# Row maxima in four groups of four heads, and value products of two heads interleaved on two column groups

## What is computed

```python
h = _layernorm(x) * (1 + ca) + sa
qkv = h @ w_qkv + b_qkv                      # 16 heads, 8 channels each
att = einsum('bhqd,bhkd->bhqk', q, k) / sqrt(8)
att = softmax(where(causal, att, -inf))
y   = einsum('bhqk,bhkd->bhqd', att, v)
x   = x + ga * (y @ w_proj + b_proj)
```

## Time and profile before

| | |
|---|---|
| timed runs | 3812.28, 3829.35, 3831.82 us |
| span of the profiled execution | 3803.2 us |
| timed runs less the span | 9.1, 26.2, 28.6 us |
| TensorE matmul busy | 3028.9 us, 80% |
| VectorE, ScalarE, GpSimd busy | 51%, 43%, 21% |
| mean granted TensorE clock | 0.854 of 2.4 GHz |

### The profile page before, as it was taken

How to read it: one execution, slowest core, us unless ns; L and a number is a source line. 1 busy time by engine, 2 the same in 40 slices (tenths; PEclk the granted TensorE clock), 3 DMA queues, 4 the chain that set the end, 5 groups by cost and what they waited for, 6 DMA issues and landing times.

```text
span 3803.2 us, 61240 instructions
## 1 busy us (share of the span) xinstructions
PE 3028.9 (80%) x21188; PEld 2136.8 (56%) x21188; DVE 1929.8 (51%) x4785; ACT 1619.0 (43%) x3753; POOL 801.2 (21%) x517
## 2 busy tenths in 40 slices
PE   1587987779787896879869799787987879887896
PEld 1255763467544674447744477354773557634685
DVE  3237643566435664356552665427653376435663
ACT  0137442464325543265423654237442374424643
POOL 0004310133103321033210432004310043102331
PEclk7688987889888997889978899788987889878897
DMA  3300012000210003001030000300003000120002
GB/s 93 66 3 13 13 23 60 3 14 14 44 38 4 15 12 79 4 3 16 9 80 4 6 15 8 80 4 9 14 16 70 3 13 13 26 58 3 14 14 37
DMA packets 228391, 96.33 MB, mean 25 GB/s; under 512 B 176114, under 2 KB 218236, under 8 KB 225668
## 3 DMA queue, kind: packets, MB, share of 16 engines
q1 hardware_dynamic: 223826, 89.88, 11.9%
q10 hardware_dynamic: 4224, 2.10, 0.2%
HBM read 70.74 MB, written 21.17 MB: 24 GB/s over the span
## 4 chain that ended last, share of the span: by engine, by line
PE 56%; ACT 15%; issue 10%; DVE 8%; DMA 5%; SPq 4%; POOL 1%; DVEq 0%; ACTq 0%; POOLq 0%
PE bank L540 7%; DMA vq<-qk_bounce 3%; PE bank L792 3%; SPq L1738 3%; PE bank L593 3%; PE bank L602 3%; PE bank L854 2%; PE bank L825 2%; PE bank L772 2%; PE bank L716 2%; PE bank L804 2%; PE bank L774 2%; PE bank L776 2%; PE bank L794 2%; PE bank L500 2%
## 5 line engine op out<-in xcount | busy, mean ns | idle before, releaser
L1658 POOL TENSOR_TENSOR arena<-upto,gk 128x1536 f32<-128x1536 f32 x32 | 88.1, 2753 | 1540.9 <-DVE beta L1139 1540.9
L500 PE MATMUL bank<-vq 72*128 72x128 bf16 (+3 forms) x512 | 189.8, 435 | 176.6 <-DMA vq<-qk_bounce 158.2
L1146 DVE SCALAR_TENSOR_TENSOR arena<-bank,conv,arena 128x510 f32<-128x510 f32 (+1 forms) x384 | 285.5, 747 | 72.8 <-ACT arena L1436 50.0
L540 PE MATMUL bank<-arena,vq 128*32 128x512 f32 (+3 forms) x1024 | 302.8, 446 | 0.0
L1036 DVE TENSOR_REDUCE mx<-bank 128x1 f32<-128x128 f32 (+3 forms) x512 | 217.0, 482 | 166.3 <-PE bank L501 162.6
L1650 POOL TENSOR_TENSOR arena<-arena 128x511 f32<-128x511 f32 x192 | 243.3, 1269 | 222.0 <-DVE arena L1146 221.9
L1401 ACT ACTIVATE arena<-bank 128x384 f32<-128x384 f32 (+1 forms) x384 | 175.8, 528 | 240.0 <-PE bank L527 240.0
L664 PE MATMUL bank<-h_t,arena 128*128 128x512 f32 x384 | 225.3, 682 | 51.3 <-DVE arena L1146 51.2
L1523 ACT COPY u<-bank 32x128 f32<-32x128 f32 x192 | 49.3, 257 | 470.9 <-PE bank L786 469.8
L500 PEld LDWEIGHTS bank<-vq 72*128 72x128 bf16 x512 | 64.9, 128 | 263.8 <-issue 174.9
L716 PE MATMUL bank<-vq 64*128 64x128 f32 x1536 | 166.6, 314 | 52.8 <-ACT arena L1510 36.5
(11 more groups left out here) (294 smaller groups left out, 7094.1 us busy)
## 6 DMA issues: line engine op xcount, KB each, us to landing
vq<-qk_bounce SPq DMA_DIRECT2D x162, 128.0 KB
arena<-w_bounce SPq DMA_DIRECT2D x16, 1024.0 KB, 16.4
qk_bounce<-arena SPq DMA_DIRECT2D x18, 384.0 KB, 2.4
arena<-in_L_attn_Wv_dram SPq DMA_DIRECT2D x8, 768.0 KB, 20.3
t<-t_bounce SPq DMA_DIRECT2D x256, 12.0 KB, 1.7
x<-t_bounce SPq DMA_DIRECT2D x256, 12.0 KB, 1.7
arena<-in_L_attn_Wq_dram SPq DMA_DIRECT2D x8, 384.0 KB, 15.1
arena<-in_L_attn_Wk_dram SPq DMA_DIRECT2D x8, 384.0 KB, 17.7
```

What stands on the lines that cost most here:

```text
L500: mm(ps[:, 0:e], q_stack[0:KS, h, t * P:e], k_stack[0:KS, h, 0:e], start=True, stop=False)
L540: last = mm(y_bank(g)[r:r + 32, j * P:T], v32[:, j, h, :], p_t[:, h % 2, c0:c0 + n], start=(j == 0), stop=(j == NT - 1))
L1146: ins = V.scalar_tensor_tensor(a[:, k:T], ps[:, 0:T - k], conv[:, n, 3 - k:4 - k], a[:, k:T], ALU.mult, ALU.add)
```

## The change

- The maxima are moved in four groups of four heads. `mparts` has two halves; the transpose always takes both (96 rows), and the SP queue sends the 48 rows of the group. `move_maxima(0)` stands behind scores 5, the others behind `scores_t` 1, 5 and 9. `mrest`, `mparts` and `m_t` change shape, the bounce buffer and the semaphores become four.
- The lead of `scores` over `scores_t` falls from 11 heads to 8.
- `weigh` takes a pair of heads: the matmul of the even head and that of the odd one alternate, key tile by key tile, in the partitions r and r + 32 of one bank. It stands behind `scores_t` of each odd head from 3 on, for the pair before. `p_t` holds four heads.
- The maxima have PSUM bank 7 for themselves and the values bank 6; `weigh` of an even pair waits for the `copy_y` before. `scores_t` alternates between two sets of banks from head 10 on (before: from head 8).
- VectorE's four splitting instructions are issued four times a pass on half the width.

```diff
-        p_t = arena[:, 0:2 * 10 * P].rearrange("p (i w) -> p i w", i=2)
+        p_t = arena[:, 0:4 * 10 * P].rearrange("p (i w) -> p i w", i=4)
-        mrest = sb("mrest", [P, HA // 2 * NT])
-        mparts = sb("mparts", [P, PARTS, HA // 2 * NT], BF16)
-        m_t = sb("m_t", [PARTS * HA // 2 * NT, P], BF16)
+        HG = HA // 4
+        mrest = sb("mrest", [P, HG * NT])
+        MR = PARTS * HG * NT
+        mparts = sb("mparts", [P, 2, PARTS, HG * NT], BF16)
+        m_t = sb("m_t", [2 * MR, 2, P], BF16)
...
-        max_banks = [PS[7], PS[6]]
+        max_bank, y_bank = PS[7], PS[6]
         def score_t_bank(h, i):
-            return PS[3 + i if h < 8 or h % 2 else i]
+            return PS[3 + i if h < 10 or h % 2 else i]
...
+                def move_maxima(g):
+                    pe.wait_ge(m_parts, at(b, m_parts, g + 1))
+                    if g == 0:
+                        pe.wait_ge(x_done, at(b, x_done, 1))
+                    else:
+                        pe.wait_ge(m_sb, at(b, m_sb, g))
+                    tr(max_bank[0:2 * MR, 0:P // 2].bitcast(BF16), mparts[:, :, :, :].rearrange("p i n m -> p (i n m)"), ident_bf[:, :]).then_inc(m_ps, 1)
...
-                        if h >= 9:
+                        if h >= 11:
                             pe.wait_ge(p_ready, at(b, p_ready, 3 * (h - 2) + i + 1))
-                        elif 1 <= h < 8:
+                        elif h == 10:
+                            pe.wait_ge(s_max, at(b, s_max, HA * NT))
+                        elif 1 <= h < 10:
                             pe.wait_ge(p_ready, at(b, p_ready, 3 * (h - 1) + i + 1))
...
+                def weigh(pair):
+                    if pair % 2 == 0 and pair:
+                        pe.wait_ge(y_sb, at(b, y_sb, pair // 2))
+                    pe.wait_ge(p_ready, at(b, p_ready, 6 * pair + 6))
                     c0 = 0
                     for j in range(NT):
                         n = T - j * P
-                        last = mm(y_bank(g)[r:r + 32, j * P:T], v32[:, j, h, :], p_t[:, h % 2, c0:c0 + n],
-                                  start=(j == 0), stop=(j == NT - 1))
+                        for h in (2 * pair, 2 * pair + 1):
+                            r = 32 * (h % 4)
+                            last = mm(y_bank[r:r + 32, j * P:T], v32[:, j, h, :], p_t[:, h % 4, c0:c0 + n],
+                                      start=(j == 0), stop=(j == NT - 1))
                         c0 += n
                     last.then_inc(pv_ps, 1)
-                for h in range(10):
-                    scores(h)
-                move_maxima(0)
-                scores(10)
-                for h in range(11, HA):
-                    scores(h)
-                    scores_t(h - 11)
-                    if h > 11:
-                        weigh(h - 12)
-                move_maxima(1)
-                for h in range(HA - 11, HA):
+                LAG = 8
+                for h in range(LAG):
+                    scores(h)
+                    if h == 5:
+                        move_maxima(0)
+                for h in range(HA):
+                    if h + LAG < HA:
+                        scores(h + LAG)
                     scores_t(h)
-                    weigh(h - 1)
-                weigh(HA - 1)
+                    if h in (1, 5, 9):
+                        move_maxima(h // 4 + 1)
+                    if h % 2 and h > 1:
+                        weigh(h // 2 - 1)
+                weigh(HA // 2 - 1)
...
                 def copy_y(g):
-                    act.wait_ge(pv_ps, at(b, pv_ps, 4 * g + 4))
+                    act.wait_ge(pv_ps, at(b, pv_ps, 2 * g + 2))
...
-                    if h == 5:
-                        copy_maxima(1)
-                    if h >= 2 and h % 4 != 1:
-                        act.wait_ge(pv_ps, at(b, pv_ps, h - 1))
+                    if h >= 4 and h % 2 == 0:
+                        act.wait_ge(pv_ps, at(b, pv_ps, h // 2 - 1))
...
-                    if h % 4 == 0 and h:
+                    if h in (1, 5, 9):
+                        copy_maxima(h // 4 + 1)
+                    if h % 4 == 1 and h > 1:
                         copy_y(h // 4 - 1)
...
-                for hh in range(2):
+                for g in range(4):
+                    sp.wait_ge(m_sb, at(b, m_sb, g + 1))
+                    sp.dma_start(m_bounce[g].rearrange("p (a t) -> (p a) t", t=P), m_t[MR * (g % 2):MR * (g % 2 + 1), g % 2, :]).then_inc(m_out, 16)
+                    sp.wait_ge(m_out, at(b, m_out, 16 * (g + 1)))
+                    sp.dma_start(q_stack[KS:KS + PARTS, HG * g:HG * (g + 1), :], m_bounce[g].rearrange("p (h t) -> p h t", t=T)).then_inc(m_in[g], 16)
```

More of the change, by code:

```diff
@@ L221, in adaln_two_layers @@
         qk_bounce = dram("qk_bounce", [2, HA, DA, PARTS, T], BF16)
-        m_bounce = dram("m_bounce", [2, PARTS, HA // 2 * T], BF16)
+        m_bounce = dram("m_bounce", [4, PARTS, HG * T], BF16)
         b_bounce = dram("b_bounce", [NBK, HD, BS, BS])
@@ L245, in adaln_two_layers @@
             "s_ps", "s_max", "m_parts", "m_ps", "m_sb", "m_out")]
-        m_in = [sig("m_in_0"), sig("m_in_1")]
+        m_in = [sig("m_in_0"), sig("m_in_1"), sig("m_in_2"), sig("m_in_3")]
         st_ps, p_ready, pv_ps, y_sb, yt_ps, y_norm, y2_ps, y2_sb, proj_ps = [sig(n) for n in (
@@ L501, in scores @@
                         mm(ps[:, t * P:e], ident_bf[:, :], mask_q[:, :], start=False, stop=True).then_inc(s_ps, 1)
-                def move_maxima(hh):
-                    pe.wait_ge(m_parts, at(b, m_parts, hh + 1))
-                    if hh == 0:
+                def move_maxima(g):
+                    pe.wait_ge(m_parts, at(b, m_parts, g + 1))
+                    if g == 0:
                         pe.wait_ge(x_done, at(b, x_done, 1))
[L507 to L510, removed]
+                    else:
+                        pe.wait_ge(m_sb, at(b, m_sb, g))
+                    tr(max_bank[0:2 * MR, 0:P // 2].bitcast(BF16), mparts[:, :, :, :].rearrange("p i n m -> p (i n m)"), ident_bf[:, :]).then_inc(m_ps, 1)
                 def scores_t(h):
-                    if h % 8 == 0:
-                        pe.wait_ge(m_in[h // 8], at(b, m_in[h // 8], 16))
+                    if h % HG == 0:
+                        pe.wait_ge(m_in[h // HG], at(b, m_in[h // HG], 16))
                     lots = [[0], [1], [2, 3]]
@@ L940, in _ @@
             V.memset(k_stack[0:PARTS, :, :], 1.0).then_inc(prologue_sb, 1)
-            V.memset(mrest[:, :], 0.0).then_inc(x_done, 1)
+            V.memset(mparts[:, :, :, :], 0.0).then_inc(x_done, 1)
             row, steps = [0], [0]
@@ L1028, in tiles @@
                     return ps[:, :].rearrange("p (c d) -> p c d", c=NT)
-                for hh in range(2):
-                    for h in range(8 * hh, 8 * hh + 8):
+                for g in range(4):
+                    for h in range(HG * g, HG * g + HG):
                         for t in range(NT):
@@ L1037, in _ @@
                             last.then_inc(s_max, 1)
[L1038 to L1042, removed]
+                    m = mx[:, HG * g:HG * (g + 1), :].rearrange("p h c -> p (h c)")
+                    dve.wait_ge(s_max, at(b, s_max, HG * NT * (g + 1)))
+                    if g:
+                        dve.wait_ge(m_ps, at(b, m_ps, g))
+                    V.tensor_scalar(mparts[:, g % 2, 0, :], m, -1.0, None, ALU.mult).then_inc(dve_step, 1)
                     dve.wait_ge(dve_step, step())
-                    V.scalar_tensor_tensor(mrest[:, :], m, -1.0, mparts[:, 0, :], ALU.mult, ALU.subtract).then_inc(dve_step, 1)
+                    V.scalar_tensor_tensor(mrest[:, :], m, -1.0, mparts[:, g % 2, 0, :], ALU.mult, ALU.subtract).then_inc(dve_step, 1)
                     dve.wait_ge(dve_step, step())
-                    V.tensor_copy(mparts[:, 1, :], mrest[:, :]).then_inc(dve_step, 1)
+                    V.tensor_copy(mparts[:, g % 2, 1, :], mrest[:, :]).then_inc(dve_step, 1)
                     dve.wait_ge(dve_step, step())
-                    V.tensor_tensor(mparts[:, 2, :], mrest[:, :], mparts[:, 1, :], ALU.subtract).then_inc(m_parts, 1)
+                    V.tensor_tensor(mparts[:, g % 2, 2, :], mrest[:, :], mparts[:, g % 2, 1, :], ALU.subtract).then_inc(m_parts, 1)
                 for t in range(NT):
@@ L1379, in layer_norm, with copy_maxima @@
                     deviation(b, k)
[L1382 to L1386, removed]
+                def copy_maxima(g):
+                    act.wait_ge(m_ps, at(b, m_ps, g + 1))
+                    if g >= 2:
+                        act.wait_ge(m_out, at(b, m_out, 16 * (g - 1)))
+                    A.copy(m_t[:, g % 2, :], max_bank[0:2 * MR, 0:P // 2].bitcast(BF16)).then_inc(m_sb, 1)
                 def copy_y(g):
-                    act.wait_ge(pv_ps, at(b, pv_ps, 4 * g + 4))
-                    A.copy(y32[:, g, :], y_bank(g)[:, :]).then_inc(y_sb, 1)
+                    act.wait_ge(pv_ps, at(b, pv_ps, 2 * g + 2))
```

(7 more changed lines are left out.)

10 lines of the change are left out of this document (4 added, 6 removed).

## The result

The changed kernel takes 3644.99 us (median of four runs, 3637.36 to 3678.06); the kernel before, run beside it, 3821.32 us. The ratio on record is 0.9582 (0.9548 to 0.9615), which is 0.0418 x 3821 = 160 us; 136 were forecast. It is not the quotient of these two medians, which is 0.9539, or 176 us. A second session gave 3666.94 against 3827.94 us, 0.9592 (0.9556 to 0.9629), 156 us; there the medians differ by 161. So the direction and the mechanism were right and the gain was 20 us or more larger than forecast. Both medians lie under the range of 3672 to 3722 us, the first by 27 us, the second by 5. The span of the changed kernel's profile is 3643.6 us, and that run took 1.7 us more.

The account below looks back on a forecast made before the run. TensorE's queue was taken to bound the kernel, value products costliest at 302.8 us. Savings of 17.0 us a pass, 136 in eight, gave a span of 3667 and a time of 3693 us, range 3672 to 3722.

Parts of the forecast that it names:

- The sum: Second pass's attention: six steps end at 654.4, not 671.36, so 17.0 us saved a pass, 136 us in eight.
- step 6: End of the attention: the last pair of heads takes 2.35 us of value products, ending at 654.4.
- the working from span to time: Timed runs lay 9 to 29 us above their span; span forecast 3667 us, against their median 3693 us.
- Two column groups side by side: Value products of two heads overlap on TensorE: a pair takes 2.35 us, bounds 2.28 and 4.56.
- the rivals at 2.74, 4.04 and 4.56 us a pair: Value products: less overlap 2.74 us (chance 0.17), weight loads not hidden 4.04 (0.03), no overlap 4.56 (0.05).
- strict order: Second head's value products start one 512-column pass late, 0.46 us: pair 2.74 us, kernel 3719 to 3740; chance 0.17.
- second rival: Weight loads of the value products are not hidden: a pair takes 4.04 us, the kernel 3802 us; chance 0.03.
- Step 1: Start of the transposed scores: maxima of fewer heads are awaited, so they start at 608.9 rather than 614.25.
- Step 2: Cold stretch before the first value products: they start at 619.5, and the clock rises 2.4 us later, at 621.9.
- Steps 4 and 5: Heads 4 to 7 take twice 6.01 us; heads 8 to 15 four times 4.11 us plus 0.55 us waiting for ScalarE.
- The reference: Second pass of the kernel before, its attention running from the first score at 591.86 to the last copy at 671.36.
- The rival of the clock: TensorE's clock stays low or falls again between value products: slower than before, 3954 us at worst; chance 0.07.

## Why the prediction was right in kind and off in size

The mechanism held; what failed are sizes. The sum's gain was 17 us too small: step 6, the cost taken for a pair, and the pass that it was scaled from. And the working from span to time left too little room for the scatter between executions. Step by step:

- *Two column groups side by side* was right, and closer to the bound than taken: 2.28 us a pair, taken 2.35. So the rivals at 2.74, 4.04 and 4.56 us a pair fall. (For strict order the prediction points at its second rival; it is the first.) The rule of the Trainium skill (TensorE: Matmul & The Clock Gate, Part 3) that weight loads overlap only with matmuls of another row group doesn't hold for these products, which use all 128 rows. The trace has the 16 loads of a pair, 0.11 us each, within the 2.28 us.
- *Step 1*: first transposed scores at 17.0 us forecast, 17.5 in the second pass, 17.7 and 16.8 in the mean of the two profiles. VectorE's pace and the round trip were read right. *Step 2*: first products at 27.6 forecast, 28.2 measured; rise at 30.0 forecast, at 29.9.
- *Steps 4 and 5*: 6.01 us forecast, 606.79 - 600.94 = 5.85 measured. Head 9's wait, forecast 0.55, was 0.45 (609.07 to 611.27 for two heads that cost 1.76). At this point the pass stands 45.3 us behind its first score, 45.5 by the sum.
- *Step 6 was mis-sized*: the last two pairs take 3.95 us, not 4.70. They are on four different column groups, and the sum held them one behind the other, though rows 8 had shown two neighbours in other groups overlap. 0.75 x 8 = 6 us.
- *The reference was mis-sized*: the pass that I scaled from ended its attention at 79.5 us, the mean of the eight is 80.3: 6 us. With these two terms and the 5 us of the pairs' 0.07 and of step 4, the 136 us become 153, which lies between the 146 and the 157 of the two profiles; these differ mostly by the start of the transposed scores, 7 us.
- *The working from span to time was wrong*. I took the 9 to 29 us between the span and the timed runs for what lies around it. That is 1.7 us; the rest is scatter between executions. The profile of before was itself a short one (3803.2 us, under each of its timed runs, 3808 to 3842 in two sessions). One part of this scatter is the wait column, 101 and 132 us for the same changed kernel. I had allowed 15 us for a run that lies low.
- *What that makes of the 3693*: the second session's 3667 lies 26 us under it, and the gain's 17 us with the 1 us by which before ran faster than 3829 leave 8. The first session's 3645 lies 48 us under it; the same 17 and a before 8 us faster (3821) leave 23. The shorter wait can hold most of these; that it does was not shown. To hold the 3645 the range had to start 27 us lower.
- *The rival of the clock* didn't come: the clock rose 1.7 us after the first product in the second pass, 1.7 to 4.3 us in all eight, and held over 3.6 us of bf16 scores. Its premise, that bf16 alone might let it fall, did not show over 6 us either, in the run with added products.

## What to carry to other kernels

Products with few weight columns cost here the stream of their moving data (from start to start, at the fast clock, 0.43 us for 512 moving columns and 0.11 for 128, with 32 weight columns; 0.11 for 128 with 128 weight columns in L836). Put those of independent heads into different column groups and interleave their instructions: here two, and even four, ran in the time of one. Look for the proof in the trace of before, at neighbours that already lie in different groups. When a stage starts at the slow clock though TensorE is busy, try a few full-array products in a wait that it has anyway, and read the granted clock per pass. And take the time of a forecast from several runs: the profile of before lay over 20 us under the median.

## What the runs showed of the hardware

- The f32 value products of four heads, with 32 weight columns each, in four column groups and 128 rows, take 2.36 us for 32 instructions; the eight instructions of one head take 2.34. The four heads overlap to within 1%.
- TensorE starts instructions for another column group ahead of earlier ones, but not far: in head-after-head order the second head gained 0.7 of 2.28 us. In the kernel before, head 15's first product starts at 668.99, ahead of three instructions of head 14 (the last at 669.52).
- 22 us of bf16 scores at 72 rows kept 1.2 GHz; 3.4 us of bf16 products at 128 rows, or 3.7 us of f32, brought 2.4 GHz, and the same scores then held it for the 6 us up to the first products.
- The same program, run twice, waited 137 and 165 us for the transfers that build the stacks.
- TensorE was busy for all of the 10.71 us from the first transposed scores to the first product at 1.2 GHz; the same stretch at 2.4 GHz took 6.15 us.
